# A transformer layer on one core: first loads in groups, the router's product by halves, three stage-end waits moved into the next stage

## The chip, the core and the metric

The kernel runs on one core of one Trainium2 chip. It is one program without the help of a scheduler: each engine (PE = TensorE, DVE = VectorE, ACT = ScalarE, POOL = GpSimd, SP = SyncE) has its own list of instructions in the order of the code, and the engines meet only at semaphores. The metric is the time of one execution on the device in microseconds (us). Before the change it is 2940.11 us, the median of 3 runs (2939.56 to 2941.16).

## What is computed

The input is x of 8 x 1024 tokens with 256 features, f32. Cut to what matters:

```python
# layer 0: gated linear attention, 4 heads
xn = layernorm(x)
q, k, v = xn @ Wq, xn @ Wk, xn @ Wv
g = maximum(log_sigmoid(xn @ Wgk1 @ Wgk2 + bgk2) / 16, -3)
o = scan(S = S * exp(g_t) + k_t v_t ; o_t = q_t S)      # over the 1024 tokens
x = x + (rmsnorm(o) * rms_w * silu(xn @ Wg)) @ Wout
# layer 1: softmax attention, 16 heads, then 8 experts, 2 for a token
y = layernorm(x)
h = y + attention(rmsnorm(y, ln1_w), wq, wk, wv, wo)
r = rmsnorm(h, ln2_w)
logits = r @ gate_w.T ; two experts and their shares by top_k and softmax
out = x + h + sum over chosen e of share_e * (silu(r @ w1[e].T) * (r @ w3[e].T)) @ w2[e].T
```

## The kernel before, in words

Five stages run one behind the other. Behind each stage stands a barrier of all engines, the stage's semaphores are cleared, and a second barrier follows (`Stage.__exit__`, lines 36 to 41). An engine reaches the barrier when its own list of the stage is done, waits at the list's end included.

**First stage** (`gla_and_projections`, names with `a_`): 16 half sequences of 512 tokens. The body for n does the tail of half n and the front of half n + 1, and transposes the input of half n + 2; n runs from -2. SP issues all loads at the start: three halves of x, then 13 weights, then `ln1_w`, the last 14 of them on one semaphore, `w_in`. PE begins with a wait for all 14, transposes the three attention weights wq, wk, wv (line 650, 12 transposes; DVE splits each into a high and a low part, lines 521 and 523), then forms Wgk1 @ Wgk2 (655, 659; DVE 525, 527), and waits for `front_done`. DVE has by then split the 1792 columns of all front weights (529, 531). Only behind it come PE's transposes of the normalised input (676), ACT's copy to `xT` (204) and the first projection, z (670). POOL writes the reciprocal root of the variance (587, 589) and behind it three memsets (626 to 628). DVE normalises in line 367. At the stage's end SP waits for the stores of x1, q, k and v.

**Second stage** (`softmax_attention`, `b_`): 64 pairs of heads. SP issues the last store of the attention output from `oT[0]` (1023) and waits for it (1026).

**Third stage** (`output_projection_and_gate`, `c_`): 16 halves of 512 tokens. PE's list in period n: output projection of half n (line 1587, 16 matmul records); transposes of the scaled rows `xg` of half n - 1 (1561); spread of the inverses for half n + 2 (1545, needs the loads `c_rd`, SP line 1317); router product of half n - 1 (1568, for each of 4 token tiles one product for each of the two feature halves k = 0, 1, 8 columns wide); places of half n - 2 (1577, 1578). ACT scales the transposed rows by `ln2` into `xgT`, one instruction for each k (1357, 1358), with one semaphore step behind the second. DVE adds `h` (1508), forms `base` (1512), and then `choose(n-1)` (copies the logits in 1441, top 8 and their indices, 1444 to 1454), `place(n-2)` (1478, 1480), `count(n-1)`, `shares(n-1)`, and the rows `xg` of half n (1526), then `oT` of half n + 1 (1425). ACT issues the stores of `base` (1362) and of `xg` (1368), and at the end waits for all of them, for `xg` in three rings `xg_st0` to `xg_st2`; half 15 is on `xg_st0`.

**Fourth and fifth stage** (`invert_places_and_transpose_weights`, `r_`, and `experts`, `d_`): the inverse of the token places, the transposed expert weights, then 136 tiles of 128 tokens.

Of the kernel before, what the change touches and what calls it, by code (L numbers as in the profile page):

```python
# [43 lines left out]
def gla_and_projections(nc, ctx, x, Wq, Wk, Wv, Wg, Wgk1, Wgk2, bgk2, Wout, rms_w,  # L44
# [87 lines left out]
    def _(sp):  # L132
        two = lambda w: w.rearrange("(k p) n -> p k n", p=P)
        loads = [(Wgk1_s[:], two(Wgk1)), (Wgk2_s[:], Wgk2), (bgk_s[:], bgk2.rearrange("(p o) -> p o", o=1)),
                 (front_raw[:, :, 128:256], two(Wq)), (front_raw[:, :, 256:384], two(Wk)),
                 (front_raw[:, :, 384:640], two(Wv)), (front_raw[:, :, 640:896], two(Wg)),
                 (Wout_s[:], two(Wout)), (rmsw_s[0:64, :], rms_w.rearrange("(p o) -> p o", o=1)),
                 (rmsw_s[64:128, :], rms_w.rearrange("(p o) -> p o", o=1)),
                 (w_raw[:, 0], two(wq)), (w_raw[:, 1], two(wk)), (w_raw[:, 2], two(wv))]
        for h in range(3):  # L140
            sp.dma_start(xin[:, h], x_v[h]).then_inc(s[f"x_in{h}"], 16)
        for dst, src in loads:
            sp.dma_start(dst, src).then_inc(s["w_in"], 16)
# [50 lines left out]
        sp.wait_ge(s["st_v"], 16 * N)  # L194

    @block.scalar
    def _(act):
# [107 lines left out]
        def values(h, pair):  # L305
# [8 lines left out]
            last.then_inc(s["v_done"], 1)  # L314

# [1909 lines left out]
```

## Time and profile before

| | |
|---|---|
| median of 3 runs | 2940.11 us |
| profiled execution | 2935.69 us |
| its span | 2934.0 us |
| PE, DVE, ACT, POOL busy | 96%, 79%, 62%, 24% of the span |
| mean granted TensorE clock | 0.967 of full |
| moved by DMA | 243.14 MB, mean 83 GB/s |

The rows below come from the profiled execution, so they add up to 2934.0 us and not to the median. Times in them are microseconds from the span's start unless marked ns. "PE" rows are matmuls, of which many f32 ones stand as two records (x16 for 8), "PEld" their weight loads. In square brackets stands how long the engine stood idle before the instruction, and what ended that. An instruction that a semaphore holds is shown from the moment it may start; one that waits inside the engine is shown as long.

### The profile page before, as it was taken

Reading aid. Unit: us, or ns where it says so; the run is one execution under the profiler, and the core shown is the slowest. Engines: PE = TensorE matmul, PEld = TensorE weight load, DVE = VectorE, ACT = ScalarE, POOL = GpSimd, SP = SyncE. Lnnn points to the kernel's source line nnn. Section 1 sums busy time; section 2 is a strip of 40 time slices with the busy share of each in tenths; the row PEclk is TensorE's granted clock in tenths of the full one; section 3 lists DMA queues with packets and bytes.
Section 4 is the critical chain, followed back from the end, with each engine's and each line's share of the span. In section 5 each row is a group of like instructions: output and inputs, shape, how many; then the busy total and the mean of one; then the engine's idle time right before and its main releaser. Section 6 shows DMA issues by size and latency. Waiting matters only on the chain. (4 is left out here: it accounts for less than half of the span.)

```text
span 2934.0 us, 64441 instructions
## 1 busy us (share of the span) xinstructions
PE 2807.6 (96%) x23285; PEld 1770.8 (60%) x23286; DVE 2332.1 (79%) x4224; ACT 1832.7 (62%) x3608; POOL 693.0 (24%) x996
## 2 busy tenths in 40 slices
PE   5999999998999999999999999999878999999997
PEld 4777777863333333333333333337767888888886
DVE  5787877778999999999999999957787656656654
ACT  3666666636888888888888888875534222222221
POOL 2233323321000000000000000001103666666564
PEclk8999999988999999999999999998889999999999
DMA  1233333332222222222222222216742333333332
GB/s 47 90 119 110 118 113 116 109 129 94 71 73 86 60 76 68 64 75 68 65 75 69 63 76 67 66 47 210 225 134 70 54 53 52 53 52 53 52 53 39
DMA packets 170751, 243.14 MB, mean 83 GB/s; under 512 B 30920, under 2 KB 118240, under 8 KB 170512
## 3 DMA queue, kind: packets, MB, share of 16 engines
q1 hardware_dynamic: 121920, 170.57, 18.9%
q0 software_dynamic: 31152, 52.33, 9.1%
q10 hardware_dynamic: 17440, 16.98, 1.8%
q8 instruction: 160, 2.62, 0.4%
q14 instruction: 79, 0.65, 0.1%
HBM read 126.53 MB, written 111.21 MB: 81 GB/s over the span
## 5 line engine op out<-in xcount | busy, mean ns | idle before, releaser
L1048 ACT ACTIVATE b_probs<-b_p_e 128x512 f32<-128x512 f32 x2048 | 1105.5, 597 | 147.8 <-PE b_p_e L1194 51.4
L1115 DVE TENSOR_REDUCE b_mxq<-b_p_m 128x1 f32<-128x1024 f32 x512 | 610.3, 1222 | 42.0 <-PE b_p_m L1142 37.4
L1115 DVE TENSOR_REDUCE mxq<-b_p_m 128x1 f32<-128x1024 f32 x496 | 591.4, 1222 | 30.8 <-PE b_p_m L1142 26.1
L1142 PE MATMUL b_p_m<-b_kst,b_qst 64*128 64x512 f32 x1024 | 377.0, 447 | 0.0
L1194 PE MATMUL b_p_e<-qst,kst 64*128 64x512 f32 x1024 | 374.3, 445 | 0.0
L1194 PE MATMUL b_p_e<-b_qst,b_kst 64*128 64x512 f32 x1024 | 373.5, 444 | 0.2 <-ACT b_probs L1048 0.2
L1142 PE MATMUL b_p_m<-kst,qst 64*128 64x512 f32 x992 | 367.6, 451 | 1.6 <-DVE b_mxq L1115 1.6
L1167 PE MATMUL b_p_o<-b_probs,b_vst 128*32 128x256 f32 x4112 | 322.0, 391 | 0.5 <-ACT b_probs L1048 0.4
L1167 PE MATMUL b_p_o<-b_probs,vst 128*32 128x256 f32 x4096 | 320.5, 390 | 0.0
L1194 PEld LDWEIGHTS b_p_e<-qst,kst 64*128 64x128 f32 x1024 | 158.2, 185 | 209.0 <-ACT b_probs L1048 177.9
L1194 PEld LDWEIGHTS b_p_e<-b_qst,b_kst 64*128 64x128 f32 x1024 | 157.5, 184 | 208.3 <-ACT b_probs L1048 177.5
L2040 DVE TENSOR_SCALAR raw<-d_p_y,raw 128x256 f32<-128x256 f32 x136 | 65.9, 485 | 259.3 <-PE d_p_y L2112 259.3
L1966 ACT COPY raw<-d_p_h 128x128 f32<-128x128 f32 x136 | 36.2, 266 | 365.8 <-PE d_p_h L2100 365.8
L1915 POOL DMA_INDIRECT out_dram<-raw x136 | 217.6, 1600 | 173.4 <-PE d_p_x L2085 81.2
L2093 PE MATMUL d_p_up<-up_hi,d_xh 128*128 x544 | 225.0, 414 | 6.8 <-issue 6.8
L2093 PE MATMUL d_p_up<-up_hi,d_xl 128*128 x544 | 214.0, 393 | 0.0
L2093 PE MATMUL d_p_up<-up_lo,d_xh 128*128 x544 | 213.9, 393 | 0.0
L1092 POOL DMA_DIRECT2D o_d<-b_oT x63 | 35.7, 567 | 658.3 <-ACT b_oT L1038 658.3
L1167 PEld LDWEIGHTS b_p_o<-b_probs,b_vst 128*32 128x32 f32 x4112 | 84.3, 108 | 163.3 <-issue 86.6
L1167 PEld LDWEIGHTS b_p_o<-b_probs,vst 128*32 128x32 f32 x4096 | 83.9, 108 | 161.4 <-issue 89.6
L1961 ACT ACTIVATE raw<-d_p_up 128x512 f32<-128x512 f32 x136 | 81.3, 598 | 144.3 <-PE d_p_up L2093 141.7
L2110 PE MATMUL d_p_y<-d_w_hi,d_hT 128*128 x816 | 168.2, 282 | 3.0 <-DVE d_hT L2033 3.0
(334 smaller groups left out, 5328.9 us busy)
## 6 DMA issues: line engine op xcount, KB each, us to landing
qk_d<-a_hi SPq DMA_DIRECT2D x32, 512.0 KB, 2.8
qk_d<-a_lo SPq DMA_DIRECT2D x32, 512.0 KB, 3.7
v_d<-a_v_s SPq DMA_DIRECT2D x16, 1024.0 KB, 4.6
o_d<-b_oT POOLq DMA_DIRECT2D x63, 256.0 KB, 2.7
qst<-qk_d SPq DMA_DIRECT2D x192, 64.0 KB, 3.1
kst<-qk_d SPq DMA_DIRECT2D x192, 64.0 KB, 2.8
b_qst<-qk_d SPq DMA_DIRECT2D x192, 64.0 KB
b_kst<-qk_d SPq DMA_DIRECT2D x192, 64.0 KB
```

What stands on the lines that cost most here:

```text
L1048: nc.scalar.activation(probs[(2 * step + e % 4 // 2) % BUFS][:, (e % 2) * 512:(e % 2 + 1) * 512], p_e[(slot(e) if more1 else e) % EB][:], ...
L1092: g.dma_start(o_rows[pair], oT[(r + 1) % 2][:]).then_inc(s["o_stored"], 16)
L1115: V_.reduce_max(mxq[half][:, h, qt:qt + 1], p_m[j % 2][:], AX.X).then_inc(s["m_red"], 1)
L1142: mm(p_m[j % 2][:, kh * 512:(kh + 1) * 512], qst[r][rows(h), qt * P:(qt + 1) * P], kst[r][rows(h), kh * 512:(kh + 1) * 512], start=True, s ...
L1167: last = mm(p_o[32 * (2 * h + a):32 * (2 * h + a) + 32, at:at + 256], vst[step // KT % RING][:, step % KT, h, :], probs[(2 * step + h) % B ...
L1194: mm(p_e[u % EB][:], kst[r][rows(h), kt * P:(kt + 1) * P], qst[r][rows(h), a * 512:(a + 1) * 512], start=True, stop=True).then_inc(s["e_ps ...
L1915: g.indirect_dma_start(out_d, bass.IndirectOffsetOnAxis(ap=to[r], axis=0), y[r], None, compute_op=ALU.add).then_inc(s[f"y_out{r}"], 16)
L1961: nc.scalar.activation(act_s, p_up[r][:, 0], ACT.Silu).then_inc(s["act_done"], 1)
L1966: nc.scalar.copy(hT_whole, p_h[:, SPLIT:4])
L2040: V_.tensor_scalar(y[q % 2], p_y[:, 0:D], share[q][:, 0:1], None, ALU.mult).then_inc(s["y_done"], 1)
L2093: last = mm(p_up[r][:, u], x[r][:, k], w[:, bass.ds(e, 1), u, k, :].rearrange("p o n -> p (o n)"), start=(j == 0), stop=(j == 5))
L2110: mm(p_y[:, 0:D], a[:, k], w[:, bass.ds(e, 1), k, :].rearrange("p o n -> p (o n)"), start=(k == 0 and j == 0), stop=False)
```

## The change

Three edits. The first gives the loads three semaphores (`gk_in`, `front_in`, `w_in`), issues the first half of x first, then the three small gate weights and the four front weights; moves the three weight transposes and their splits to places in the bodies -1 and 0; lets ACT round 1536 of the 1792 front columns; moves PE's wait for `front_done` behind the first input transposes; and puts the memset of `AT` ahead of POOL's root and those of `Sbd` and `v_s` behind `front_done`. The second gives `xgT` a semaphore step for each k, turns the router's loops (k outside, t inside), and puts the places of half n - 2 before the router product on PE and before `choose` on DVE. The third keeps `v_s`, `oT[0]` and `xg[0]` outside their stages' memory, so that their last stores may still be under way when the stage ends; the wait for each stands in the next stage. Some small tiles of the fourth stage are laid into `hi_tiles`.

```diff
@@ -131,15 +132,16 @@
     @block.sync
     def _(sp):
         two = lambda w: w.rearrange("(k p) n -> p k n", p=P)
-        loads = [(Wgk1_s[:], two(Wgk1)), (Wgk2_s[:], Wgk2), (bgk_s[:], bgk2.rearrange("(p o) -> p o", o=1)),
-                 (front_raw[:, :, 128:256], two(Wq)), (front_raw[:, :, 256:384], two(Wk)),
-                 (front_raw[:, :, 384:640], two(Wv)), (front_raw[:, :, 640:896], two(Wg)),
-                 (Wout_s[:], two(Wout)), (rmsw_s[0:64, :], rms_w.rearrange("(p o) -> p o", o=1)),
-                 (rmsw_s[64:128, :], rms_w.rearrange("(p o) -> p o", o=1)),
-                 (w_raw[:, 0], two(wq)), (w_raw[:, 1], two(wk)), (w_raw[:, 2], two(wv))]
-        for h in range(3):
+        sp.dma_start(xin[:, 0], x_v[0]).then_inc(s["x_in0"], 16)
+        for dst, src in ((Wgk1_s[:], two(Wgk1)), (Wgk2_s[:], Wgk2), (bgk_s[:], bgk2.rearrange("(p o) -> p o", o=1))):
+            sp.dma_start(dst, src).then_inc(s["gk_in"], 16)
+        for dst, src in ((front_raw[:, :, 128:256], two(Wq)), (front_raw[:, :, 256:384], two(Wk)),
+                         (front_raw[:, :, 384:640], two(Wv)), (front_raw[:, :, 640:896], two(Wg))):
+            sp.dma_start(dst, src).then_inc(s["front_in"], 16)
+        for h in (1, 2):
             sp.dma_start(xin[:, h], x_v[h]).then_inc(s[f"x_in{h}"], 16)
-        for dst, src in loads:
+        for dst, src in ((w_raw[:, 0], two(wq)), (w_raw[:, 1], two(wk)), (w_raw[:, 2], two(wv)), (Wout_s[:], two(Wout)),
+                         (rmsw_s[0:64, :], rms_w.rearrange("(p o) -> p o", o=1)), (rmsw_s[64:128, :], rms_w.rearrange("(p o) -> p o", o=1))):
             sp.dma_start(dst, src).then_inc(s["w_in"], 16)
         with nc.allow_non_contiguous_dma("256 weights, once"):
             sp.dma_start(ln1w_s[:], ln1_w.rearrange("(k p) -> p k", p=P)).then_inc(s["w_in"], 16)
...
@@ -191,7 +193,6 @@
         sp.wait_ge(s["st_x1"], 16 * N)
         sp.wait_ge(s["st_q"], 32 * N)
         sp.wait_ge(s["st_k"], 32 * N)
-        sp.wait_ge(s["st_v"], 16 * N)
 
     @block.scalar
     def _(act):
@@ -312,6 +313,9 @@
                 last = A.copy(v_s[:, :, t, :].rearrange("p a (h e) -> p a h e", h=2)[:, :, :, 0:16],
                               p_g[:, 2 + pair, (t % 2) * D:(t % 2 + 1) * D].rearrange("p (a h e) -> p a h e", a=8, h=2))
             last.then_inc(s["v_done"], 1)
+
+        act.wait_ge(s["front_in"], 4 * 16)
+        A.copy(W_f[0][:, :, 128:896], front_raw[:, :, 128:896]).then_inc(s["w_hi"], 1)
 
         for n in bodies:
...
-        statistics(0)
-        normalise(0)
-        for j in range(3):
+        def weights(j):
+
             dve.wait_ge(s["wT_ps"], j + 1)
             out = [w[:, j].rearrange("p k m -> p (k m)") for w in wT]
-            V_.tensor_copy(out[0], p_g[:, j]).then_inc(s["wT_hi"], 1)
+            V_.tensor_copy(out[0], p_g[:, 2 + j % 2]).then_inc(s["wT_hi"], 1)
             dve.wait_ge(s["wT_hi"], j + 1)
-            V_.tensor_tensor(out[1], p_g[:, j], out[0].bitcast(f32), ALU.subtract).then_inc(s["wT_done"], 1)
+            V_.tensor_tensor(out[1], p_g[:, 2 + j % 2], out[0].bitcast(f32), ALU.subtract).then_inc(s["wT_done"], 1)
+
+        statistics(0)
         dve.wait_ge(s["gk_ps"], 1)
         V_.tensor_copy(Wgk1T[:], p_g[0:16, 3, 0:D]).then_inc(s["gk1T_done"], 1)
+        normalise(0)
         dve.wait_ge(s["gk_ps"], 2)
         V_.tensor_copy(front_raw[:, :, 0:128], p_g[:, 3, 0:D].rearrange("p (k m) -> p k m", k=2)).then_inc(s["raw_done"], 1)
         dve.wait_ge(s["raw_done"], 1)
-        V_.tensor_copy(W_f[0][:], front_raw).then_inc(s["front_hi"], 1)
+        V_.tensor_copy(W_f[0][:, :, 0:128], front_raw[:, :, 0:128]).then_inc(s["front_hi"], 1)
         dve.wait_ge(s["front_hi"], 1)
+        dve.wait_ge(s["w_hi"], 1)
         V_.tensor_tensor(W_f[1][:], front_raw, W_f[0][:].bitcast(f32), ALU.subtract).then_inc(s["front_done"], 1)
 
         for n in bodies:
             input_low(n + 1)
+            if n == 0:
+                weights(1)
             first_maxima(n, (0, 1))
...
+            if n == 0:
+                weights(2)
             layer_norm(n - 1)
             gate_minimum(n + 1)
...
+            if n == -1:
+                weights(0)
             first_maxima(n, (8, 9))
             rests(n, (0,))
...
+        g.memset(AT[:], 0.0)
         front_root(0)
-        g.memset(AT[:], 0.0)
+        pool.wait_ge(s["front_done"], 1)
         g.memset(Sbd[:], 0.0)
         g.memset(v_s[:], 1.0).then_inc(s["filled"], 1)
...
         mm, tr = nc.tensor.matmul, nc.tensor.transpose
-        pe.wait_ge(s["w_in"], 14 * 16)
         pe.wait_ge(s["consts"], 1)
-        for j in range(3):
-            for k in range(2):
-                for m in range(2):
-                    last = tr(p_g[:, j, k * D + m * P:k * D + (m + 1) * P], w_raw[:, j, m, k * P:(k + 1) * P], ident[:])
-            last.then_inc(s["wT_ps"], 1)
-        pe.wait_ge(s["wT_done"], 3)
-
+        pe.wait_ge(s["gk_in"], 3 * 16)
         for k in range(2):
             last = tr(p_g[0:16, 3, k * P:(k + 1) * P], Wgk1_s[:, k, :], ident[:])
         last.then_inc(s["gk_ps"], 1)
@@ -658,7 +665,17 @@
         for k in range(2):
             last = mm(p_g[:, 3, k * P:(k + 1) * P], Wgk1T[:, k * P:(k + 1) * P], Wgk2_s[:], start=True, stop=True)
         last.then_inc(s["gk_ps"], 1)
-        pe.wait_ge(s["front_done"], 1)
+
+        def weights(j):
+
+            if j == 0:
+                pe.wait_ge(s["w_in"], 7 * 16)
+            if j > 1:
+                pe.wait_ge(s["wT_done"], j - 1)
+            for k in range(2):
+                for m in range(2):
+                    last = tr(p_g[:, 2 + j % 2, k * D + m * P:k * D + (m + 1) * P], w_raw[:, j, m, k * P:(k + 1) * P], ident[:])
+            last.then_inc(s["wT_ps"], 1)
 
         def product(out, wide, x, w, low_ready=None):
...
+                if f == 0:
+                    pe.wait_ge(s["front_done"], 1)
                 pe.wait_ge(s["xT_done"], f + 1)
             else:
...
+            if h == 0:
+                pe.wait_ge(s["wT_done"], 3)
             if h > 0:
...
+            if n == 0:
+                weights(2)
             projection(n + 1, "z", 2, "z_ps")
...
+            if n == -1:
+                weights(0)
+                weights(1)
             attention_projection(n, 0)
...
+        self.v_s = ctx.enter_context(nc.sbuf_tensor("v_s", [128, 8, 4, 64], f32, side="right"))
+        self.st_v = nc.alloc_semaphore("st_v")
...
-    oT = [sb(f"oT{r}", [P, 512]) for r in range(2)]
+    oT = [ahead.last, sb("oT1", [P, 512])]
...
                     sp.wait_ge(s["zrow_set"], 1)
+                if pair == 5:
+                    sp.wait_ge(pair0.st_v, 16 * 2 * n_batches)
                 load(pair + 3, (r + 3) % RING)
...
         sp.wait_ge(s["ahead_o"], 128)
-        sp.wait_ge(s["o_last"], 16)
 
     @block.scalar
...
 
+        sp.wait_ge(ahead.o_last, 16)
         for a in (0, 1):
...
             act.wait_ge(s["xgT_ps"], n + 1)
-            nc.scalar.mul(xgT[:, 0], p3[:, 0], ln2[:, 0:1])
+            nc.scalar.mul(xgT[:, 0], p3[:, 0], ln2[:, 0:1]).then_inc(s["xgT_done"], 1)
...
-        for r in range(3):
+        for r in (1, 2):
             act.wait_ge(s[f"xg_st{r}"], 16 * len(range(r, N, 3)))
...
             dve.sem_inc(s["in_free"], 1)
-            if before:
-                choose(n - 1)
             if n > 1:
                 place(n - 2)
             if before:
+                choose(n - 1)
                 count(n - 1)
                 shares(n - 1)
...
         def router(n):
-            pe.wait_ge(s["xgT_done"], n + 1)
-            for t in range(T):
-                for k in range(2):
-                    i = mm(p4[:, t, :], xgT[:, k, t * P:(t + 1) * P], gwT[:, k, :], start=(k == 0), stop=(k == 1))
+            for k in range(2):
+                pe.wait_ge(s["xgT_done"], 2 * n + k + 1)
+                for t in range(T):
+                    i = mm(p4[:, t, :], xgT[:, k, t * P:(t + 1) * P], gwT[:, k, :], start=(k == 0 and t == 0), stop=(k == 1), skip_group_check=True)
             i.then_inc(s["lg_ps"], 1)
 
...
                 spread(n + 2, half, b + 1)
+            if n > 1:
+                places(n - 2)
             if before:
                 router(n - 1)
-            if n > 1:
-                places(n - 2)
         halves(pe, body)
         router_transposes(N - 1, 1)
...
+        sp.wait_ge(rows.stored0, 16 * len(range(0, NT // 4, 3)))
 
```

What follows is the order of PE's instructions at the start of the program. The names are outputs and inputs; `a_lo` holds the raw attention weights, `a_Wgk_s` the gate weights, `a_xn` the normalised input. Before:

```order
L650 MATMUL a_p_g<-a_ident,a_lo 128x128 x12
L655 MATMUL a_p_g<-a_ident,a_Wgk_s 16x128 x2
L659 MATMUL a_p_g<-a_Wgk_s,a_Wgk1T 128x128 x2
L676 MATMUL a_p_f<-a_ident,a_xn 128x128 x8
L670 MATMUL a_p_f<-a_xT,a_W_f 128x512 x4
```

And now, with the later place of the moved transposes behind the "...":

```order
L662 MATMUL a_p_g<-a_ident,a_Wgk_s 16x128 x2
L666 MATMUL a_p_g<-a_Wgk_s,a_Wgk1T 128x128 x2
L693 MATMUL a_p_f<-a_ident,a_xn 128x128 x8
L687 MATMUL a_p_f<-a_xT,a_W_f 128x512 x4
...
L755 MATMUL a_p_f<-a_V,a_khat 32x64 x64
L677 MATMUL a_p_g<-a_ident,a_lo 128x128 x8
L693 MATMUL a_p_f<-a_ident,a_xn 128x128 x8
...
L773 MATMUL a_p_g<-a_V,a_AT 128x64 x4
L677 MATMUL a_p_g<-a_ident,a_lo 128x128 x4
L687 MATMUL a_p_f<-a_xT,a_W_f 128x512 x4
```

Eight of the twelve transposes moved between the state increments of half 0 and the input transposes of half 1, four between the outputs of half 0 and the projection z of half 1.

One period of the third stage on PE before, from the output projection on (`c_woT,c_oT` the output projection, `c_rd,c_heads` the spread, `c_gwT,c_xgT` the router, `c_cum` and `c_hot` the places):

```order
L1587 MATMUL c_p<-c_woT,c_oT 128x256 x8
L1561 MATMUL c_p<-ident,c_xg 128x128 x8
L1545 MATMUL c_p<-c_rd,c_heads 128x512 x2
L1568 MATMUL c_p<-c_gwT,c_xgT 128x8 x8
L1577 MATMUL c_p<-c_cum,ones_r 128x64
L1578 MATMUL c_p<-c_hot,lower_r 128x64
```

And now:

```order
L1631 MATMUL c_p<-c_woT,c_oT 128x256 x8
L1605 MATMUL c_p<-ident,c_xg 128x128 x8
L1589 MATMUL c_p<-c_rd,c_heads 128x512 x2
L1621 MATMUL c_p<-c_cum,ones_r 128x64
L1622 MATMUL c_p<-c_hot,lower_r 128x64
L1612 MATMUL c_p<-c_gwT,c_xgT 128x8 x8
```

The two products of the places moved from behind the router's products to the front of them.

## Rows read from the trace of the kernel before

**Rows 1.** Timeline, opening of the program (start us, length us, engine, line; idle before).

```profile
3.61 0.41 DVE L347 CAST a_maski<-a_o 128x512 int32<-128x512 f32 x1 [2.01 <-issue]
...
4.99 1.40 DVE L355 BATCH_NORM_STATS2 a_st<-a_xin 128x6 f32<-128x256 f32 x4 [0.97 <-DMA a_xin<-in_L_attn_x_dram]
...
8.31 8.03 DVE L367 TENSOR_SCALAR a_xn<-a_xin,a_mv,a_rstd 128x256 f32<-128x256 f32 x4 [1.50 <-POOL a_rstd L589]
...
13.43 1.80 POOL L628 MEMSET a_v_s<- 128x2048 f32 x1
...
14.11 2.82 PE L650 MATMUL a_p_g<-a_ident,a_lo 128*128 128x128 f32 x12 [14.11 <-DMA a_ln1w_s<-in_L_ffn_ln_w_dram]
...
19.62 0.69 DVE L523 TENSOR_TENSOR a_wT<-a_p_g,a_wT 128x512 fp32r<-128x512 f32 x1
...
22.72 0.42 DVE L527 COPY a_hi<-a_p_g 128x256 f32<-128x256 f32 x1 [1.31 <-PE a_p_g L659]
...
24.31 2.03 DVE L531 TENSOR_TENSOR a_W_f<-a_hi,a_W_f 128x1792 fp32r<-128x1792 f32 x1
...
26.39 1.97 PE L676 MATMUL a_p_f<-a_ident,a_xn 128*128 128x128 f32 x8 [3.71 <-DVE a_W_f L531]
...
28.39 1.01 ACT L204 CAST a_xT<-a_p_f 128x1024 fp32r<-128x1024 f32 x1 [26.31 <-PE a_p_f L676]
...
29.46 2.07 PE L670 MATMUL a_p_f<-a_xT,a_W_f 128*128 128x512 f32 x4 [1.10 <-ACT a_xT L204]
```

**Rows 2.** One line's instructions, DVE L367 (ns min/median/max), whole program.

```profile
L367 DVE TENSOR_SCALAR a_xn<-a_xin,a_mv,a_rstd x64: 397/407/7074, 8.3 to 561.9; 128x256 f32<-128x256 f32 x64
```

**Rows 3.** Timeline, PE before the second input transposes.

```profile
56.64 0.66 PE L676 MATMUL a_p_f<-a_ident,a_xn 128*128 128x128 f32 x2 [5.44 <-DVE a_S L498]
```

**Rows 4.** Timeline, end of the first stage.

```profile
663.36 0.36 SPq L159 DMA_DIRECT2D v_d<-a_v_s  x1
...
664.50 0.16 DVE L479 SCALAR_TENSOR_TENSOR norm<-a_mvb,a_roots 128x4 f32<-128x4 f32 x1
```

**Rows 5.** Waits of the SP queue (us in total, times, longest), whole program.

```profile
SPq L194 <- DMA v_d<-a_v_s: 4.0, 1, 4.0
...
SPq L1026 <- DMA o_d<-b_oT: 1.7, 1, 1.7
```

**Rows 6.** Timeline, PE, one period of the third stage.

```profile
2095.58 0.73 PE L1545 MATMUL c_p<-c_rd,c_heads 32*128 32x512 f32 x2
...
2097.01 1.95 PE L1568 MATMUL c_p<-c_gwT,c_xgT 128*128 128x8 f32 x16 [0.69 <-ACT c_xgT L1358]
...
2098.81 0.28 PE L1577 MATMUL c_p<-c_cum,ones_r 128*128 128x64 f32 x1
...
2099.04 0.68 PE L1587 MATMUL c_p<-c_woT,c_oT 128*128 128x256 f32 x2
```

**Rows 7.** Timeline, ACT, same period of the third stage.

```profile
2095.69 0.69 ACT L1357 ACTIVATE c_xgT<-c_p,c_ln 128x512 f32<-128x512 f32 x1 [4.28 <-PE c_p L1561]
```

**Rows 8.** Busy time by windows in the third stage (length; engines; PEclk, DMA share, GB/s).

```profile
1990.33:2124.93 134.60, 121.43 (x610) 100.38 (x611) 104.75 (x432) 74.06 (x211) 17.72 (x28) 0.85 0.73 222
...
2057.78:2069.09 11.31, 10.62 (x45) 8.73 (x45) 8.27 (x32) 5.28 (x16) 1.26 (x2) 0.70 0.83 213
...
2069.09:2077.72 8.63, 7.51 (x44) 6.12 (x45) 6.72 (x32) 5.24 (x16) 1.27 (x2) 1.00 0.69 225
...
2087.36:2097.01 9.65, 8.96 (x45) 7.35 (x45) 7.55 (x32) 5.22 (x15) 1.26 (x2) 0.82 0.70 223
```

**Rows 9.** Waits in the third stage, 1971.5 to 2142.3 us (total, times, longest).

```profile
PE c_p L1568 <- ACT c_xgT L1358: 11.7, 16, 1.4
...
PEld c_p L1545 <- DMA c_rd<-rd_d: 0.8, 2, 0.5
```

**Rows 10.** Timeline, last store of the third stage.

```profile
2141.98 0.37 ACTq L1368 DMA_DIRECT2D xg_d<-c_xg  x1
```

**Rows 11.** All stores of line L1368, issue to landing.

```profile
DMA to landing us min/median/max: 3.2/8.6/9.3
```

More of the change, by code:

```diff
@@ L1243, in __init__ @@
         self.x1 = [sb(f"x1{r}", [P, 4, D]) for r in range(2)]
+        self.last, self.o_last = sb("last", [P, HT]), nc.alloc_semaphore("o_last")
     @staticmethod
@@ L1251, in o_rows, with __init__, output_projection_and_gate @@
         return d.rearrange("b g (h a e) q -> b a (g h) e q", h=2, a=2)
-def output_projection_and_gate(nc, ctx, ahead, o_d, rd_d, x1_d, norm, out_d, xg_d, ones_r, lower_r, slots, counts, w1, w3, w2, raw, n_batches=8):
+class RowTiles:
+    def __init__(self, nc, ctx):
+        P, T, D, f32 = 128, 4, 256, mybir.dt.float32
+        self.xg0 = ctx.enter_context(nc.sbuf_tensor("xg0", [P, T, D + 2], f32, side="right"))
+        self.stored0 = nc.alloc_semaphore("xg_st0")
+def output_projection_and_gate(nc, ctx, ahead, rows, o_d, rd_d, x1_d, norm, out_d, xg_d, ones_r, lower_r, slots, counts, w1, w3, w2, raw, n_batches=8):
     P, D, T, NE = 128, 256, 4, 8
@@ L1273, in output_projection_and_gate @@
     h, y = sb("h", [P, T, D]), sb("y", [P, T, D])
-    base, xg = [sb(f"base{r}", [P, T, D]) for r in range(2)], [sb(f"xg{r}", [P, T, D + 2]) for r in range(3)]
+    base, xg = [sb(f"base{r}", [P, T, D]) for r in range(2)], [rows.xg0, *(sb(f"xg{r}", [P, T, D + 2]) for r in range(1, 3))]
     sq, ms, r_s = sb("sq", [P, D]), sb("ms", [P, T]), sb("r_s", [P, T])
@@ L1601, in _, with invert_places_and_transpose_weights @@
         places(N - 1)
-def invert_places_and_transpose_weights(nc, ctx, ident, ones_r, lower_r, slots, counts, raw, token_of, pick, expert_of, w1, w3, w2, up_hi, up_lo, w2T, NT, TILES):
+def invert_places_and_transpose_weights(nc, ctx, rows, ident, ones_r, lower_r, slots, counts, raw, token_of, pick, expert_of, w1, w3, w2, up_hi, up_lo, w2T, NT, TILES):
     P, D, I, NE = 128, 256, 512, 8
@@ L1648, in invert_places_and_transpose_weights @@
     s = {n: stage_semaphore(nc, ctx, "r_" + n) for n in names}
+    ctx.semaphores.append(rows.stored0)
     block = ctx.enter_context(nc.Block())
@@ L2183, in layer_kernel @@
             first.close()
+            kept = ExitStack()
+            rows = RowTiles(nc, kept)
             with Stage(nc) as stage:
-                output_projection_and_gate(nc, stage, ahead, o_d, rd_d, x1_d, norm, out_d, xg_d, ones_r, lower_r, slots, counts, w1, w3, w2, raw, B)
+                output_projection_and_gate(nc, stage, ahead, rows, o_d, rd_d, x1_d, norm, out_d, xg_d, ones_r, lower_r, slots, counts, w1, w3, w2, raw, B)
         with ExitStack() as weights:
@@ L2192, in layer_kernel @@
             with Stage(nc) as stage:
-                invert_places_and_transpose_weights(nc, stage, ident, ones_r, lower_r, slots, counts, raw, token_of, pick, expert_of, w1, w3, w2, up_hi, up_lo, w2T, NT, TILES)
+                invert_places_and_transpose_weights(nc, stage, rows, ident, ones_r, lower_r, slots, counts, raw, token_of, pick, expert_of, w1, w3, w2, up_hi, up_lo, w2T, NT, TILES)
             down.close()
+            kept.close()
             with Stage(nc) as stage:
```

22 lines of the change are left out of this document (14 added, 8 removed).

## The prediction, made before the changed kernel ran

> **What bounds the kernel now.** I read the timeline of the opening first, then the SP queue's waits, then one period of the third stage, since the change touches nothing else. The opening [rows 1]: PE's first product waits until 14.11 us for the last of fourteen loads. The normalised input is made in 8.03 us from 8.31 on, but PE turns to it only at 26.39, behind the weight transposes, the gate product and DVE's split of the front weights (ends 24.31 + 2.03). The first projection starts at 29.46. Until then nearly everything is a chain, so what leaves it comes off the time. The stage ends [rows 4, 5]: SP waits 4.0 us for the last store of v and 1.7 us for the last store of the attention output, with nothing else running. The third stage [rows 6 to 8]: fourteen periods from 1990.33 to 2124.93 take 134.60 us, 9.61 each. In a period of 9.65 PE is busy 8.96 and DVE 7.55 [rows 8]; PE's one wait is for ACT's `xgT`, 0.69 in the row shown and 11.7 us over 16 [rows 6, 9]. So PE with that wait is the bound there.
>
> **The opening.** Removed from the path: the wait for all loads, 12 transposes, DVE's six splits (the last starts at 19.62, 0.69 long), and the place of the gate product ahead of the input. New, step by step:
>
> The memset of `AT` now starts where POOL's last mask instruction ends, which is when DVE's `maski` cast starts, 3.61. It is as large as that of `v_s`, 1.80 [rows 1]. Line 367 shows what a memset does to such a DVE instruction: 407 ns is its median, 7074 ns its longest [rows 2], the one of 8.31, which ended with POOL's last memset (13.43 + 1.80 = 15.23) [rows 1]. If the cast is held likewise, it ends at about 5.4 and the statistics start then and not at 4.99: 0.45 later. With the first half of x first in the queue as before, its landing isn't later than 4.99. Normalising then starts at 8.31 + 0.45 = 8.76. Without a memset beside it its four instructions take 1.3 (8.03 - 7.07 = 0.96 for the last three): 10.05. PE's transposes take 1.97 (12.05), and ACT's copy starts right behind them and lets the projection start 1.07 after that (29.46 - 28.39): 13.15.
>
> Second branch: DVE copies the gate product (0.42), casts 256 columns (estimate 0.3), subtracts over all columns (2.03): 10.05 + 2.9 = 12.95, just ahead of 13.15. Its inputs: the gate product was 1.31 after DVE's last need [rows 1], small loads issued second, so it falls beside the normalising. ACT's cast of 1536 columns is 1.4 to 1.5 (1024 take 1.01 [rows 1]); the front loads are issued by about 5.1, and the first load of x needed 4.2 to land (4.99 - 0.80); with as much or half as much again they are there by 9.3 to 11.4, the cast done at 10.8 to 12.9. I take the early end; the late one costs 1.9. So z starts at 13.15 and not at 29.46: **-16.3**. Behind `front_done`, POOL's memsets run for 5.3 beside DVE's first instructions of the loop. `Sbd` and `v_s` are needed only 18 us behind z. If they held DVE as they held line 367, that would cost up to 5.3; but what runs there (a subtraction from PSUM, statistics, a scaled add from PSUM) is of other kinds, and I take 0. Together the bounds are -9.1 and -16.8 (cast not held).
>
> The skill speaks to both memsets. The row says a memset held line 367 for its whole length and those behind it [rows 1, 2]. The Trainium skill (SBUF — State Buffer, "SBUF: two separate sides") says that a GpSimd instruction and a VectorE instruction in a two-port mode exclude each other, whoever starts first holding the ports for its whole instruction, while a VectorE instruction with two SBUF inputs clashes only with a GpSimd one that reads SBUF. The trace agrees with the first half (7074 ns). It speaks against moving `AT` forward, the 0.45 above; by its second half the later memsets cost nothing.
>
> Moved, not removed: eight transposes stand before the second input transposes, where PE idles 5.44 us [rows 3] and they need about 1.9: hidden; without that cover they cost 1.9. DVE's splits for them (0.68 + 0.69 each pair) stand where DVE waits for those same input transposes and for the outputs. The last four transposes stand before the projection z of half 1, on a PE list that is full: 12 took 2.82 [rows 1], so four take 0.9; **+1.0**, bounds 0.5 and 2.4 (if DVE's 1.4 counts too).
>
> **The stage ends.** First: the v store is issued at 663.36 and done being issued at 663.72; SP waits 4.0, to 667.7. DVE's last instruction ends at 664.66 [rows 4], so the barrier can close there: **-3.0**. Its wait now stands in SP's list of pair 5, long after. Second: SP waits 1.7 for a store that it issued itself, and everyone else is done: **-1.7**. The wait stands in front of the loads of `sums`, nothing on PE's first path, and the store lands as the next stage starts. Third: the last store of `xg` is issued at 2141.98, for 0.37 [rows 10], and lands 3.2 later, the shortest of its line [rows 11]: 2145.2 - 2142.35 = **-2.8**. Each could be 0 if another wait took its place; the next ones are seen and are earlier, so I don't expect it.
>
> **The third stage's periods.** In the period shown [rows 6, 7] ACT's first half of `xgT` is ready at 2095.69 + 0.69 = 2096.38, and PE's router product starts at 2097.01, with the second half. With its own step it can start at about 2096.43, behind the spread (2095.58) and the places, which now fill that gap; the second half is ready long before the first half's products (about 0.9) are through: 0.58. The places no longer stand between router and output projection (2098.81 to 2099.04): 0.23. DVE's `place` goes before its wait for the logits, so DVE's chain is shorter too. So 0.81 a period, 14 times: **-11.3**; the last half's router gains the 0.58 too: **-0.6**. Bounds: 0.3 a period if the `c_rd` loads come late (-4), and 1.8 if DVE alone is left as the bound (-25).
>
> **Sum.** -16.3 + 1.0 - 3.0 - 1.7 - 2.8 - 11.3 - 0.6 = -34.7. Against the profiled execution (2935.7) that is 2901.0. The median before is 4.4 above it, so I take the gain from the median: 2940.1 - 34.7 = 2905.4, rounded 2905.
>
> **Rivals.**
> *The clock in the third stage rises* (0.13). The granted clock is 0.85 over the fourteen periods, and the one period at 1.00 took 8.63 [rows 8]. PE has less idle time now. With the clock full, DVE bounds: 104.75 / 14 = 7.5 busy, some 7.8 with its gaps: (9.61 - 7.8) x 14 = 25.3 in place of 11.3, 2891. Against it: PE was already busy 93% of its time at 0.82.
> *The loads of the third stage become the bound* (0.12). PE's weight loads already waited for `c_rd` twice, 0.8 in all [rows 9], and the DMA share is 0.73 [rows 8], 0.80 with shorter periods. If half of a microsecond comes back as a wait in each, the gain is 4.2 in place of 11.3: 2912.
> *The opening gives less* (0.11): the memsets hold DVE, or the front loads land late: up to 7 less, 2912.
> *Slower* (0.03): the clock in the third stage falls. It went down to 0.70 in the period of 11.31 [rows 8]. The rest of the change brings 23.4, or 1.67 for each of 14 periods, so from a mean period of 11.3, a granted clock of about 0.70 all through, the kernel is slower. At half clock all through a period would be 2 x 7.51 = 15.0: +75 - 23 = 2992. For it: it has been there once, over a whole period. Against it: thirteen others were above, and no idle time is added anywhere.
>
> **Chances.** The forecast 0.60, the rest as named, 0.01 for what I don't see. The range 2892 to 2917 takes in both kinds of 2912 and all of the clock's rise but its end. A measurement of this kernel can tell about 0.2%, 5.9 us, from no change. All cases but the fall of the clock are faster by more: faster 0.95, same 0.02, slower 0.03.
>
> **What would show it.** The first z projection at about 13.2; `maski` cast of about 1.8; line 367's successor at 0.4 each; in the opening no DVE instruction of over 2.1 behind `front_done`. The second stage starts 3 us sooner behind the issue of v's last store; the router product with no wait, or one under 0.2, and periods of 8.6 to 8.9 at a clock of 0.8 to 0.9; the `xg` store still under way when the fourth stage starts. The forecast is wrong if periods stay over 9.3, if z starts after 16, or if one of the three barriers closes as late as before.

## The result, and the profile after

| | before | after |
|---|---|---|
| median | 2939.84 us (4 runs beside it, 2935.26 to 2941.16) | 2902.71 us (4 runs, 2896.95 to 2907.63) |
| profiled execution | 2935.69 | 2907.63 |
| its span | 2934.0 | 2905.9 |
| mean granted TensorE clock | 0.967 | 0.967 |

The ratio is 0.9881, with a 95% interval of 0.9868 to 0.9894: 35 us less (31 to 39). The profiled execution of the changed kernel is the slowest of its four, so the spans differ by only 28.1. The sum by places in these two traces:

| | predicted | the two profiles |
|---|---|---|
| z starts at 13.57, not 29.46 | -16.3 | -15.9 |
| from there to v's last store: 639.75, not 633.90 | +1.0 | +5.9 |
| v's last store to the second stage's first product: 4.17, not 7.55 | -3.0 | -3.4 |
| last attention store to the third stage's first product: 2.05, not 3.65 | -1.7 | -1.6 |
| from there to the first router product: 17.08, not 18.76 | 0 | -1.7 |
| fourteen periods: 126.19, not 134.60 | -11.3 | -8.4 |
| the rest of the stage: 15.02, not 15.90 | -0.6 | -0.9 |
| last third-stage product to the fourth stage's first: 3.62, not 6.24 | -2.8 | -2.6 |
| the last two stages | 0 | +0.5 |
| sum | -34.7 | -28.1 |

The opening of the changed kernel, in order of time (start, duration, engine, line, operation, idle time before and what ended it). It answers to [rows 1]:

```profile
3.50 1.79 POOL L638 MEMSET a_AT<- 128x2048 f32 x1
3.61 1.97 DVE L351 CAST a_maski<-a_o 128x512 int32<-128x512 f32 x1 [2.01 <-issue]
5.62 1.40 DVE L359 BATCH_NORM_STATS2 a_st<-a_xin 128x6 f32<-128x256 f32 x4
8.94 1.38 DVE L371 TENSOR_SCALAR a_xn<-a_xin,a_mv,a_rstd 128x256 f32<-128x256 f32 x4 [1.21 <-POOL a_rstd L602]
9.91 1.47 ACT L318 CAST a_W_f<-a_hi 128x1536 fp32r<-128x1536 f32 x1 [7.83 <-DMA a_hi<-in_L_attn_Wg_dram]
10.38 1.97 PE L693 MATMUL a_p_f<-a_ident,a_xn 128*128 128x128 f32 x8 [1.37 <-DVE a_xn L371]
11.49 2.02 DVE L538 TENSOR_TENSOR a_W_f<-a_hi,a_W_f 128x1792 fp32r<-128x1792 f32 x1 [0.50 <-ACT a_W_f L318]
12.38 1.01 ACT L205 CAST a_xT<-a_p_f 128x1024 fp32r<-128x1024 f32 x1 [1.00 <-PE a_p_f L693]
13.57 2.08 PE L687 MATMUL a_p_f<-a_xT,a_W_f 128*128 128x512 f32 x4 [1.22 <-DVE a_W_f L538]
13.57 3.52 POOL L641 MEMSET a_Sbd<- 128x4096 f32 x1 [4.67 <-DVE a_W_f L538]
14.57 1.39 DVE L359 BATCH_NORM_STATS2 a_st<-a_xin 128x6 f32<-128x256 f32 x4
```

The `maski` cast, 0.41 before, takes 1.97 beside `AT`'s memset and ends 0.3 behind it. Normalising takes 1.38 and not 8.03. Two chains then end within 0.15 of each other: xT at 13.39 and the weights' subtraction at 13.51. The statistics beside the later memset take 1.39, as those before them do, so nothing is held there.

The first instructions of the second and of the fourth stage on PE, in the changed kernel; they answer to [rows 4, 10]:

```profile
657.49 0.37 PE L1179 MATMUL b_p_e<-b_ident,b_hl 128*32 128x128 f32 x1 [4.27 <-POOL b_hl L1102]
...
2118.45 0.59 PE L1839 MATMUL r_p_s<-counts,r_ones 128*128 128x8 f32 x2 [3.62 <-DVE r_ones L1737]
```

v's last store is issued at 653.32 and lands at 657.81, the last one of `xg` is issued at 2115.97 and lands at 2119.04: both are still under way when the next stage's PE starts. SP's two waits of [rows 5] are gone from its list.

The third stage of the changed kernel by windows (columns as in [rows 8]; a period runs from one router product to the next): the fourteen periods, and four of them.

```profile
1973.62:2099.81 126.19, 117.75 (x614) 97.87 (x613) 107.25 (x433) 74.09 (x211) 17.71 (x28) 0.86 0.79 236
1973.62:1984.17 10.55, 10.55 (x46) 8.92 (x45) 7.98 (x31) 5.44 (x16) 1.27 (x2) 0.68 0.67 164
1984.17:1992.53 8.36, 7.45 (x47) 6.12 (x46) 7.21 (x31) 5.41 (x16) 1.26 (x2) 1.00 0.71 251
1992.53:2002.16 9.63, 8.94 (x46) 7.33 (x46) 8.75 (x33) 5.86 (x18) 1.26 (x2) 0.82 0.92 237
2002.16:2011.04 8.88, 8.88 (x47) 7.35 (x46) 7.24 (x32) 4.49 (x15) 1.26 (x2) 0.81 0.79 237
```

And its waits over the fourteen periods (total us, times, longest), which answer to [rows 9]:

```profile
PEld c_p L1605 <- DVE c_xg L1570: 5.5, 5, 1.2
PEld c_p L1589 <- DMA c_rd<-rd_d: 4.1, 4, 1.2
PE c_p L1605 <- DVE c_xg L1570: 3.5, 5, 0.8
PE c_p L1589 <- DMA c_rd<-rd_d: 3.2, 4, 1.0
PE c_p L1612 <- ACT c_xgT L1402: 1.3, 2, 0.6
```

Before, over its own fourteen periods, the router's wait was:

```profile
PE c_p L1568 <- ACT c_xgT L1358: 9.3, 14, 1.4
```

So it has shrunk from 9.3 us to 1.3 (the 11.7 of [rows 9] is that of the whole stage). Three kinds of period stand in its place: 8.85 to 8.91 at a clock of 0.81, four times, where PE is busy nearly all the time; 9.63 to 9.95 at 0.82 to 0.83, four times, where the DMA share is 0.9 and PE waits for `c_rd`; and 7.95 to 8.37 at full clock, five times, where what PE waits for is mostly DVE's `xg`. The one left is the first, 10.55 at 0.68.

### The profile page after: what moved, and what is told of

Its sections match the earlier page's. It is cut to its first block and busy times, and to the rows that moved or that the text cites. A ratio compares the mean times of both kernels' runs of the same rounds, so it can differ in the third digit from the quotient of the medians.

```text
span 2905.9 us, 64449 instructions
## 1 busy us (share of the span) xinstructions
PE 2806.5 (97%) x23285; PEld 1769.8 (61%) x23286; DVE 2327.4 (80%) x4224; ACT 1835.0 (63%) x3609; POOL 693.4 (24%) x996
## 5 line engine op out<-in xcount | busy, mean ns | idle before, releaser
L1173 PEld LDWEIGHTS b_p_m<-b_kst,b_qst 64*128 64x128 f32 x1024 | 155.2, 184 | 7.7 <-DVE b_mxq L1146 3.2
```

The source lines that it names most:

```text
L1173: mm(p_m[j % 2][:, kh * 512:(kh + 1) * 512], qst[r][rows(h), qt * P:(qt + 1) * P], kst[r][rows(h), kh * 512:(kh + 1) * 512], start=True, s ...
```

## The experiments

The changed lines are shown against the kernel named. "First stage" is the time from z to v's last store. The runs come from four chips, and the kernel before ran beside each group, with medians of 2938.41 (the first four runs), 2932.22 (`e5` to `e8_best`), 2939.56 (`after_again`, `e8_again`, `e10`) and 2936.11 (`e11`); so medians of different groups are compared by their ratios.

**The three edits one at a time.** Each was put alone on the kernel before.

*Opening alone.*

> Only the opening edit, on the kernel before. Own price (theory): z starts at 13.6 us and not at 29.46, that is 15.9 earlier, and nothing else of the program changes; the time falls by 16, less what the granted clock does in the first stage (0 to 6 in one execution). Its sixteen halves then obey the same table as before: 36.2 us at a granted clock of 1.00, 37.2 at 0.95, 38.8 at 0.91. Rival (the moved transposes, splits and memsets cost work in the first stage): halves are longer than that at the same granted clock, by some 6 us in all, in the first three halves above all, and the time falls by 10 in every execution.

Median 2925.78 beside 2938.41, ratio 0.9958 (0.9943 to 0.9973). z starts at 13.55. The adds to x1 of the first three halves come 16.1, 16.2 and 16.2 earlier than before. The halves keep to the table, 36.2 at a clock of 1.00, 37.2 at 0.95, 38.8 at 0.91, but for the fourth and the tenth, which are longer in the kernel before too. The moved work costs nothing there, and the rival falls by the halves; by the time it doesn't, since the interval, 8 to 17 us less, holds both. It is -12.6 in the median and -13.5 in the profile: the first stage took 1.6 more than in the profile before, the third stage's periods 2.2 less, and the fifth stage 2.0 more (705.3, not 703.4), each with its granted clock.

*Third stage alone.*

> Only the router product by halves of the features and the places ahead of it, on the kernel before. Theory: the third stage's fourteen periods take 9.0 each and not 9.61, the tail 0.9 less: -9.3, and nothing in the stages before moves. Periods alternate by granted clock and load: 8.9 at 0.82, about 8.4 at 1.00, 9.6 where PE waits for c_rd. Rival (the periods gained only because the stage started at another place of the clock's cycle): under -5. Rival (the unexplained 1.7 us between the stage's first product and its first router product comes from this edit too): -11.

Median 2928.93, ratio 0.9971 (0.9962 to 0.998). The periods:

```profile
1992.15:2119.28 127.13, 117.72 (x613) 97.84 (x613) 107.27 (x433) 74.00 (x211) 17.76 (x28) 0.87 0.79 234
```

9.08 each, where the kernel before has 9.61 and the two with the old order here (`e1`, `e3`) have 9.46 and 9.52. The tail is 0.9 less, the head 0.6 less, the whole stage 8.9. So the edit brings about as much alone as in the full change, and of the head's 1.7 it brings 0.6. The profile before is the longest of three with the old order (134.60, 132.39, 133.26, mean 133.4); six with the edit and the old order of the loads took 126.05 to 127.13, mean 126.3. The fairer price is 7.1, or 0.51 a period.

*Stage ends alone.*

> Only the three last stores waited for in the next stage, on the kernel before. Theory: -3.4 at the first barrier, -1.6 at the second, -2.6 at the third: -7.6. Rival (the laying of small tiles of the fourth stage into hi_tiles, or a store that is still under way beside the next stage's loads, gives part of it back): -5 or less, with the fourth stage or the head of the third longer than 75.4 us and 18.8 us.

Median 2927.72, ratio 0.9966 (0.9954 to 0.9978). The barriers bring 3.4, 1.6 and 2.6, the fourth stage keeps its length, nothing is given back. The head of the third stage is 1.1 shorter, which I had not expected of it. The windows of its first outputs and of the whole head, first of before, then of this kernel:

```profile
1971.57:1981.70 10.13, 10.13 (x27) 6.68 (x27) 5.24 (x12) 2.05 (x4) 0.73 (x6) 0.55 0.50 144
1971.57:1990.33 18.76, 16.28 (x54) 11.02 (x55) 11.37 (x23) 7.37 (x19) 2.01 (x8) 0.76 0.45 136
```

```profile
1967.63:1976.65 9.02, 9.02 (x26) 5.87 (x26) 5.23 (x12) 2.06 (x4) 0.74 (x6) 0.62 0.53 125
1967.63:1985.29 17.66, 15.20 (x55) 10.28 (x55) 11.37 (x23) 7.38 (x19) 2.02 (x8) 0.80 0.53 144
```

PE is busy in every microsecond of the first window in both, and it is 1.1 shorter at a clock of 0.62 than at 0.55. So the 1.1 is the granted clock's. PE stood idle for 2.7 us ahead of the stage and not for 4.3. Every profile has the same pairs: behind 2.7 the head takes 17.1, or 17.7 without the halves; behind 4.2 to 4.3 it takes 18.8 and 19.1, or 18.2 with them.

**The third stage's new limits.**

*The loads.* Changed kernel with

```diff
-                load_output(half, b + 1)
                 load_inverses(half, b + 1)
+                load_output(half, b + 1)
```

> The changed kernel with SP's loads of the inverses c_rd issued ahead of those of the attention output c_oin. Theory (loads bound every third period of the third stage: PE waits up to 1.0 for c_rd in four of fourteen, with a period of 9.6 to 9.95 where 8.9 would be due): those waits go, -3 to -4 against the changed kernel, about 2899 to 2900 by its median. Rival (DVE's product waits for c_oin instead, which now is issued 0.9 later): no gain, and DVE waits for c_oin in those periods. Rival (all loads of such a period are late since the stores of xg fill the queues): c_rd lands as late as before, no gain.

```profile
1971.02:2095.46 124.44, 116.25 (x614) 96.79 (x613) 107.66 (x433) 73.94 (x211) 17.70 (x28) 0.88 0.83 240
1989.92:1998.79 8.87, 8.87 (x46) 7.37 (x46) 8.00 (x33) 5.10 (x16) 1.26 (x2) 0.81 0.86 248
```

No wait for `c_rd` is left, no period at 0.81 is above 8.9, and DVE doesn't wait for `c_oin`. But the gain is 1.75 and not 3 to 4. Two periods at a clock of 0.68 took 10.5 each, where the changed kernel has one, and each is 1.7 longer than one at 0.81. The later `e8_again`, with the same order of loads and one such period, took 122.64, which is 3.55 less. The median, 2901.44 (ratio 0.9873, 0.9857 to 0.989), can't tell the difference.

*The halves.* Changed kernel with one semaphore step for both halves of `xgT`, and PE's loops turned back:

```diff
-            for k in range(2):
-                pe.wait_ge(s["xgT_done"], 2 * n + k + 1)
-                for t in range(T):
+            pe.wait_ge(s["xgT_done"], n + 1)
+            for t in range(T):
+                for k in range(2):
```

> The changed kernel with the router's product back to one semaphore step and tokens outside, places still ahead of it. Theory (the halves are worth 0.58 in a period that PE sets, nothing where DVE or c_rd sets it): periods at a granted clock of 0.81 to 0.82 rise from 8.88 to about 9.4, those at 1.00 from 8.37 to at most 8.6, mean 9.3; +4 against the changed kernel, about 2907. Rival (the places already fill the wait, so the halves bring nothing): mean period 9.0, no difference. First stage as in the changed kernel: if its 639.75 us from z to v's last store were chance of the granted clock, this execution gives another figure, between 634 and 640, with the same pairs of clock and time for each half; if they were a cost of the change, 639 to 640 again.

```profile
1977.18:2106.86 129.68, 121.02 (x613) 100.35 (x613) 107.05 (x432) 74.00 (x211) 17.71 (x28) 0.86 0.75 230
1988.18:1997.61 9.43, 9.07 (x45) 7.46 (x45) 7.73 (x32) 5.25 (x16) 1.26 (x2) 0.82 0.70 231
1997.61:2006.28 8.67, 7.64 (x44) 6.18 (x44) 6.99 (x32) 5.24 (x16) 1.27 (x2) 1.00 0.73 251
```

This gives both prices. At a clock of 0.82 a period takes 9.42 (eight of the fourteen; one took 9.67). The places ahead of the router are worth 9.64 - 9.42 = 0.22 and the halves 9.42 - 8.88 = 0.54 where PE sets the period. The mean is 9.26, so of those 0.54 only 0.25 come out in the changed kernel. PE waits for `c_rd` here too, but less:

```profile
PE c_p L1589 <- DMA c_rd<-rd_d: 1.4, 3, 0.7
```

Only the period with the 0.7 is longer for it (9.67); the other two, with 0.3 and 0.4, took 9.41 and 9.42 like the rest. In the changed kernel the same wait comes to 3.2 in four periods, and all four are longer: the shorter the period, the more the loads cost. The first stage took 642.68, not 639.75. Median 2910.94 (ratio 0.991, 0.9883 to 0.9938), an interval that meets the changed kernel's.

**The opening's terms.**

*AT's memset behind front_done too.* Changed kernel with

```diff
-        g.memset(AT[:], 0.0)
         front_root(0)
         pool.wait_ge(s["front_done"], 1)
+        g.memset(AT[:], 0.0)
```

> The changed kernel with the memset of AT behind front_done as well. Theory: the maski cast is no longer held (0.41 and not 1.97), the input is normalised 0.5 earlier, xT is ready 0.5 earlier, but z stays at 13.5 to 13.6, since DVE's subtraction for the front weights waits for ACT's cast, and that for the last front load. Rival (the opening's chain through the input alone sets z): z at 13.0.

```profile
3.61 0.41 DVE L351 CAST a_maski<-a_o 128x512 int32<-128x512 f32 x1 [2.01 <-issue]
4.64 1.41 DVE L359 BATCH_NORM_STATS2 a_st<-a_xin 128x6 f32<-128x256 f32 x4 [0.62 <-DMA a_xin<-in_L_attn_x_dram]
10.47 2.03 DVE L538 TENSOR_TENSOR a_W_f<-a_hi,a_W_f 128x1792 fp32r<-128x1792 f32 x1 [0.47 <-ACT a_W_f L318]
12.56 2.06 PE L687 MATMUL a_p_f<-a_xT,a_W_f 128*128 128x512 f32 x4 [1.19 <-DVE a_W_f L538]
```

z starts at 12.56, 1.0 earlier, against my theory. x lands by 4.64, so the memset cost the input's chain 1.0. But the last front load landed 1.0 earlier here too (ACT's cast starts at 8.89), and z needs both. With the load as late as in the changed kernel's first profile, where the subtraction ended at 13.51, z would have stayed at 13.6, as the theory said. Over the profiles of this study that cast starts between 8.3 and 10.0: the load's moment varies, and the late memset brings between 0 and 1.0 by it. One execution, 2903.18.

*All memsets where they were.* Changed kernel with

```diff
-        g.memset(AT[:], 0.0)
         front_root(0)
-        pool.wait_ge(s["front_done"], 1)
+        g.memset(AT[:], 0.0)
```

> The changed kernel with all three memsets where they were, behind POOL's first root, with no wait for front_done. Theory (a memset holds a tensor-scalar instruction of DVE from SBUF to SBUF for as long as the memsets run): normalising takes 8.0 and not 1.38, z starts 6 to 7 later, at about 20. Rival (the placement of the memsets doesn't matter, since the loads of the front weights set z): z under 14.

```profile
7.82 8.03 DVE L371 TENSOR_SCALAR a_xn<-a_xin,a_mv,a_rstd 128x256 f32<-128x256 f32 x4 [1.20 <-POOL a_rstd L602]
```

z starts at 19.07, 5.5 later. The hold is shown, and it is a third of what the opening brings. Yet this execution took 2907.64, just what the profiled one of the changed kernel took: its first stage took 634.36 and not 639.75, so v's last store is issued at 653.43, beside 653.32 there. Beside the changed kernel's second profile (649.56, next paragraphs) it is 3.9 late. One execution can't price an edit of this size.

**Is the loss in the first stage a cost of the change?** The changed kernel once more:

> The changed kernel once more, unchanged. Theory (what the first profile gave back in the first stage is chance of the granted clock): z at 13.6 again, the third stage's periods 9.0 again, but another figure than 639.75 us from z to v's last store, between 632 and 643, with each half at 36.2, 37.2 or 38.8 for a clock of 1.00, 0.95 or 0.91. Rival (a cost of the change): 639 to 640 again. The median within 2898 to 2906.

z at 13.54, periods of 9.00, median 2901.70, ratio 0.987 (0.9849 to 0.989). The first stage took 636.02. Three halves of the first profile show what sets its length (third column from the right is the clock):

```profile
104.03:141.23 37.20, 36.99 (x359) 29.69 (x358) 29.48 (x70) 23.63 (x44) 11.29 (x12) 0.95 0.33 114
290.84:327.09 36.25, 35.69 (x359) 28.48 (x358) 28.64 (x69) 23.72 (x44) 11.05 (x12) 1.00 0.34 117
476.79:515.58 38.79, 38.57 (x359) 30.86 (x358) 28.62 (x70) 23.63 (x44) 12.21 (x13) 0.91 0.32 109
```

The work is the same (359 matmul records each), the time goes by the granted clock. Without the new opening the three profiles show 633.90, 635.34 and 636.47; with it and with the front weights subtracted in one instruction, seven show 639.75, 636.02, 635.51, 637.25, 642.68, 636.75 and 634.36. The rival, 639 to 640 each time, falls. The means are 635.2 and 637.5, so a cost of some 2 us is neither shown nor excluded.

**A better version.** `c_rd` first and AT's memset late, as above, and the gate columns' subtraction apart:

```diff
-        dve.wait_ge(s["w_hi"], 1)
-        V_.tensor_tensor(W_f[1][:], front_raw, W_f[0][:].bitcast(f32), ALU.subtract).then_inc(s["front_done"], 1)
+        V_.tensor_tensor(W_f[1][:, :, 0:128], front_raw[:, :, 0:128], W_f[0][:, :, 0:128].bitcast(f32), ALU.subtract).then_inc(s["front_done"], 1)
+        dve.wait_ge(s["w_hi"], 1)
+        V_.tensor_tensor(W_f[1][:, :, 128:896], front_raw[:, :, 128:896], W_f[0][:, :, 128:896].bitcast(f32), ALU.subtract).then_inc(s["front_done"], 1)
```

with PE's wait for the second step ahead of the first q product, and POOL's memsets behind it.

> A version meant to beat the changed kernel: c_rd loads ahead of c_oin; AT's memset behind front_done; DVE subtracts the 256 gate columns of the front weights alone and lets z start, the other 1536 behind it. Theory: z at 12.9 to 13.0 (xT ready then) and not 13.57, q not later than before; no wait for c_rd in the third stage, its periods 8.87 at a clock of 0.81 and 8.37 at 1.00; -0.6 and -2 to -4 against the changed kernel, 2899. Rival (DVE's one large subtraction is now in the way of xTl, z's low terms wait and all that was won is lost): z's first product earlier but q's at the same time, gain of the opening 0.

> The version with c_rd loads first, AT's memset late and the gate columns apart, once more, beside the changed kernel on the same chip. By the traces it is 0.9 faster in the opening and 1.8 in the third stage, 2.7 in all; its median differed by 5.9. Theory: the difference of the medians is 2 to 4 on the mean and drowned in what the clock of the first stage does (10 us between executions). Rival (it keeps the first stage's clock up): its first stage takes 632 again and the median is 6 or more below.

Medians 2896.84 (ratio 0.9867, 0.9845 to 0.9889) and 2897.09 (0.9862, 0.9842 to 0.9882). The nine executions have a mean of 2896.6, the eight of the changed kernel 2902.0. The difference is 5.4, with a standard error of 1.6 worked out from the two spreads (3.0 and 3.6). That mixes chips; the four and four executions on one chip differ by 4.1, with a standard error of 2.2, which is less than two of these. z starts at 12.64 and 12.47. The third stage's periods took 8.88 and 8.76. That is about 1 and 2 to 3.5 us, most of the difference. The first stage took 631.94 and 631.88 us, less than in any profile without the split.

*The scaled rows earlier.* The same version, with DVE's `xg` of half n ahead of `count` and `shares` of half n - 1:

> The same version, with DVE's scaled rows xg of half n ahead of count and shares of half n - 1. Theory (at a granted clock of 1.00 DVE's chain to xg sets the period of 8.37: PE waits 0.8 to 1.2 for it, and the rows could start 1.1 earlier, when POOL's root is done): periods at 1.00 fall to 7.7 to 8.0, those at 0.81 stay at 8.87; -3 in the third stage, PE's wait for xg gone. Rival (DVE's whole list sets the period, not its order): 8.3 again. Rival (PE, with no idle time left, is granted the lower clock more often, and the gain goes there): periods at 1.00 shorter but fewer, mean 8.9.

Median 2896.58, ratio 0.9858 (0.9836 to 0.9881). Four of the seven periods at full clock took 8.45, not 7.7 to 8.0, and the fourteen took 124.4 in all, beside 124.4 and 122.6 without this edit. The waits of the fourteen periods show what came in place of `xg`:

```profile
PE c_p L1593 <- DVE c_oT L1473: 6.2, 5, 1.3
...
DVE c_xg L1571 <- POOL c_r_s L1398: 5.0, 8, 1.9
...
PE c_p L1609 <- DVE c_xg L1571: 1.9, 2, 1.1
```

The wait for `xg`, 6.1 in `e8_best`, is down to 1.9, but DVE now waits for POOL's root, its `oT` comes later, and PE waits 6.2 for that. The theory fell; moving one link only moved the wait. 8.45 is near the 8.3 of the first rival (DVE's whole list), but DVE itself stood waiting for 5.0, so its list alone isn't the bound either.

*The split alone*, on the changed kernel:

> The changed kernel with the gate columns' subtraction apart, and nothing else (AT's memset early, c_oin first). The three profiles of the versions with this split show 631.9 us from z to v's last store, those of seven kernels without it 634 to 643. Theory (the split itself shortens the first stage, since PE goes on from z to q without a gap and the clock's full level comes at another moment): 632 here too, z at 13.4, median about 2898. Rival (it is where z starts, together with AT's late memset, or chance): 634 to 643, median 2901 to 2903, z at 13.4.

The profile speaks for the theory: the first stage took 631.39, as in the three others with the split (631.88 to 631.96). The median speaks for the rival: 2902.22, ratio 0.9881 (0.9865 to 0.9898), like the changed kernel's, and the profiled execution was the shortest of the four. It stays open whether the split gives the first stage more of the clock. z came at 13.55, not 13.4, held by `xT` alone.

## Why the prediction was right

**The opening: right, and 0.4 off.** The chain ran as worked out, with `maski` held 1.97 (1.8 expected), normalising 1.38, the transposes 1.97, the copy 1.01. z came at 13.57 and not at 13.15 since each step was a little late: 5.62 for 5.44, 8.94 for 8.76, 10.38 for 10.05. The hold's price was set against x landing at 4.99; it landed by 4.45 to 4.73 in the profiles with the late memset, so the early one costs the input's chain some 1.0 and not 0.45. The front loads landed between the two ends that I gave: ACT's cast was done at 11.38, the subtraction ended at 13.51, 0.1 behind `xT`, and so they cost z next to nothing. That the later memsets would hold nothing was right; where the gate arithmetic came to stand beside one, in the better version (`e8_best`), that was no longer so:

```profile
18.10 1.82 POOL L643 MEMSET v_s<- 128x2048 f32 x1
...
19.23 0.97 DVE L415 TENSOR_SCALAR a_zm<-a_zm 128x512 f32<-128x512 f32 x1
```

Line 415, SBUF to SBUF with one source, took 0.97 there and 0.43 in the changed kernel; line 398, of the same operation but from PSUM, took 0.75 with a memset beside it and without, and line 413, with two inputs from SBUF, 0.69 with one (18.50 in `e8_best`) and without. By the Trainium skill (SBUF — State Buffer, "SBUF: two separate sides"), GpSimd and a VectorE instruction in a two-port mode exclude each other. The 8.03 of line 371 in `e7`, the 1.97 of the cast and this 0.97 agree, though no row here shows an instruction's mode.

**The moved weight transposes: half, and given back.** The last four took 0.71 (from 53.87 to 54.58), and z of half 1 is 15.4 earlier instead of 15.9. But its first products run at a higher clock than before, and the add to x1 of half 1 is 16.05 earlier. The +1.0 was 0.5 and nothing was left of it.

**The stage ends: right.** -3.4, -1.6 and -2.6 for -3.0, -1.7 and -2.8, and the same when alone.

**The third stage: the mechanism right, the size 3 too large.** The step that failed is "So 0.81 a period, 14 times". The price of 0.81 was read in one period, in which PE sets the pace and the clock is 0.82, and there it was nearly right: 0.22 for the places and 0.54 for the halves make 0.76. I multiplied it by all fourteen. The two profiles by kinds of period, number and mean length:

| | before | after |
|---|---|---|
| clock 0.68 to 0.70 | 2, 11.19 | 1, 10.55 |
| clock 0.81 to 0.83, loads in time | 8, 9.64 | 4, 8.88 |
| the same, PE waits for late `c_rd` | none | 4, 9.74 |
| full clock | 4, 8.77 | 5, 8.23 |

Two of the full-clock periods of before, and the shortest of after:

```profile
2011.04:2019.81 8.77, 7.52 (x45) 6.12 (x45) 6.83 (x32) 5.27 (x16) 1.26 (x2) 1.00 0.74 249
2048.74:2057.78 9.04, 7.53 (x45) 6.12 (x45) 6.83 (x32) 5.42 (x16) 1.27 (x2) 1.00 0.72 244
```

```profile
2029.06:2037.01 7.95, 7.46 (x47) 6.12 (x46) 6.34 (x31) 4.87 (x15) 1.26 (x2) 1.00 0.77 264
```

In four periods the loads of `c_rd` came late. They are 0.86 longer than the four others at that clock, which is more than the whole gain. That was my second rival, which I put at all periods or none. At full clock a period gained 0.54 and not 0.81, and PE waits for DVE's `xg` there; the bound of 7.8 was too low, the shortest took 7.95. Against this, the profile after has one slow period less and one at full clock more, which is worth 11.19 - 8.77 = 2.4. No experiment shows that the change does that: `e1` and `e3`, with the old order, have one slow period as well. The first rival, the clock, hardly moved on the mean (0.85 to 0.86). The mean period of 9.01 lies above the 8.6 to 8.9 that was to show the forecast, and below the 9.3 that was to refute it.

**The head of the third stage** was not in the sum: -1.7. The router's halves serve the first router product too (0.6), and behind the shorter idle time ahead of the stage the granted clock was higher (1.1).

**The sum.** Without the first stage's clock, the profiled terms are -15.9 - 3.4 - 1.6 - 1.7 - 8.4 - 0.9 - 2.6 = -34.5; the forecast was -34.7. Here the terms that fell short (the periods by 2.9, the opening by 0.4, others by 0.3) and those that brought more (the head 1.7, the transposes 1.0, others 0.7) cancel, and that is luck. So, as far as is known, is the 2.4 of the mix of periods. The median went down by 37.1. The three edits alone make 12.6 + 9.5 + 10.7 = 32.8, each uncertain by some 3 to 4.5.

## What to carry to other kernels

Read a loop's gain from each kind of its periods, not from one: split them by granted clock and by what is waited for last, price the edit in each kind, and count them. When the bound is nearly shared, the loads' order in the queue and the next engine's chain take part of it: here 0.81 was forecast for each period and some 0.5 to 0.6 came. And price an edit of a few microseconds from the interval of the trace in which it acts, with a second profile of the same code: the kernel's own spread was 10 us.

## What was not expected

- The first stage, nearly the same instructions in all kernels, took 631 to 643 us in fourteen profiles, nearly every half by its granted clock; by that chance a start 5.5 us later was made up by the stage's end beside one profile, and 1.6 of it beside another.
- A stage that starts after 2.7 us of idle PE and not after 4.3 ran its first window at 0.62 and not 0.55, and was 1.1 us shorter.
- The landing of the same front load moved by 1.7 us between profiles (ACT's cast from 8.3 to 10.0).
